# A conditioned two-layer block: weight rounding, row norms and layer gates put in another order

## The reference, cut to what matters

```python
def _weight_quant(w):
    scale = 1.0 / clip(mean(abs(w)), 1e-05)
    return clip(round(w * scale), -1, 1) / scale
def _bitlinear(x, w, nw, b=None):
    xn = x * rsqrt(mean(square(x)) + 1e-08) * nw
    y = act_quant(xn) @ weight_quant(w).T              # act_quant: 8 bits by the row's maximum
    return y if b is None else y + b
# the conditioning chain, on 2 rows
h = _bitlinear(silu(c), wa0, na0)
h = _hgrn_mlp(h, wa1, na1, wa2, na2)
h = _rmsnorm(_bitlinear(h, wa3, na3, ba3), wr, 1e-06)
s_msa, sc_msa, g_msa, s_mlp, sc_mlp, g_mlp = split(_bitlinear(h, wa4, na4, ba4), 6)
# the first mixer
mx = _layernorm(x) * (1 + sc_msa) + s_msa
f = sigmoid(_bitlinear(mx, wf, nf))
i = silu(_bitlinear(mx, wi, ni)) * (1 - f)
o = _rmsnorm(scan(i, f), gn) * silu(_bitlinear(mx, wg, ng))
x = x + g_msa * _bitlinear(o, wo, no_)
mlp_in = _layernorm(x) * (1 + sc_mlp) + s_mlp
x = x + g_mlp * _hgrn_mlp(mlp_in, wm1, nm1, wm2, nm2)  # then layer 1: attention and MLP
# layer 1: mod = silu(c) @ Wada + bada; sh_a, sc_a, gt_a, sh_m, sc_m, gt_m = split(mod, 6)
```

## Time and profile before

| | us |
|---|---|
| median of 3 runs | 249.67 (249.2 to 250.05) |
| the profiled execution | 250.22 |
| its span in the trace | 248.0 |
| VectorE, TensorE, ScalarE, GpSimd busy | 173.0, 180.0, 152.2, 78.4 |

### The profile page before, as it was taken

The page is one execution under the profiler, slowest core; times in us unless marked ns, Lnnn a source line. Parts: engine busy times, 40 slices in busy tenths (PEclk is TensorE's granted clock), DMA queues, the critical chain, the costliest instruction groups (busy, mean ns, idle before and its releaser), DMA issues.

```text
span 248.0 us, 4504 instructions
## 1 busy us (share of the span) xinstructions
PE 180.0 (73%) x1635; PEld 106.3 (43%) x1639; DVE 173.0 (70%) x501; ACT 152.2 (61%) x334; POOL 78.4 (32%) x116
## 2 busy tenths in 40 slices
PE   0223269586494659755976897699999999889894
PEld 0202226454341313311643454367556655544663
DVE  1778787999986496697697479578778777462511
ACT  3767983679724757695515642567657755976241
POOL 9261520404713013378313978011001101130120
PEclk9999999779859779995999799599999999999999
DMA  5999000000000000000000333124000000000011
GB/s 145 409 425 348 4 0 0 0 3 1 0 0 1 3 0 0 1 0 0 0 3 13 106 79 62 41 31 66 5 2 5 3 5 5 1 4 0 0 45 42
DMA packets 4635, 11.50 MB, mean 46 GB/s; under 512 B 1283, under 2 KB 2788, under 8 KB 3974
## 3 DMA queue, kind: packets, MB, share of 16 engines
q1 hardware_dynamic: 3654, 10.03, 12.1%
q0 software_dynamic: 960, 1.19, 2.0%
HBM read 8.23 MB, written 0.52 MB: 35 GB/s over the span
## 4 chain that ended last, share of the span: by engine, by line
DVE 35%; PE 29%; ACT 14%; POOL 13%; issue 6%; DMA 1%; SPq 0%; DVEq 0%; ACTq 0%; POOLq 0%
DVE negmax L1351 7%; PE ps L1747 6%; POOL uh L465 4%; PE ps L1506 4%; POOL KS L348 3%; ACT PT L793 2%; PE ps L1686 2%; PE ps L1783 2%; ACT xhat L683 2%; DVE mx L1243 2%; DVE u L1130 2%; POOL rms L405 2%; PE ps L1727 2%; PE ps L1777 1%; PE ps L1474 1%
## 5 line engine op out<-in xcount | busy, mean ns | idle before, releaser
L1351 DVE TENSOR_REDUCE negmax<-ps 128x1 f32<-128x384 f32 (+3 forms) x96 | 51.2, 593 | 14.1 <-PE ps L1688 13.8
L793 ACT ACTIVATE PT<-ps 128x1024 f32<-128x1024 f32 x40 | 39.5, 1031 | 20.4 <-PE ps L1733 20.3
L1517 PE MATMUL ps<-k_b 128*128 128x512 bf16 x114 | 33.4, 453 | 9.5 <-DVE prod L1289 4.4
L1686 PE MATMUL ps<-KS,QS 48*128 48x128 bf16 (+3 forms) x128 | 31.4, 315 | 1.6 <-DVE negmax L1351 0.8
L1727 PE MATMUL ps<-QS,KS 51*128 51x512 bf16 (+3 forms) x128 | 24.6, 311 | 1.8 <-DMA QS<-nmT 1.8
L405 POOL TENSOR_TENSOR rstd<-veps,mhalf 128x4 f32<-128x4 f32 x8 | 9.8, 1220 | 50.7 <-DVE veps L912 40.8
L1517 PEld LDWEIGHTS ps<-k_b 128*128 128x128 bf16 x114 | 12.7, 115 | 27.7 <-issue 8.9
L1687 PE MATMUL ps<-k_b 64*128 64x128 bf16 x128 | 23.8, 225 | 0.0
L1688 PE MATMUL ps<-k_b 64*128 64x64 bf16 x128 | 21.4, 195 | 0.0
L1747 PE MATMUL ps<-PT,V 128*9 128x512 f32 (+3 forms) x256 | 20.4, 434 | 0.0
L1733 PE MATMUL ps<-k_b 64*128 64x128 bf16 x128 | 18.7, 223 | 0.0
(11 more groups left out here) (237 smaller groups left out, 457.2 us busy)
## 6 DMA issues: line engine op xcount, KB each, us to landing
w<-in_wa SPq DMA_DIRECT2D x2, 1152.0 KB, 9.5
lw<-in_l_w SPq DMA_DIRECT2D x1, 1280.0 KB
brow<-in_bcast_rows SPq DMA_DIRECT2D x1, 1152.0 KB, 15.4
mw<-in_main_w SPq DMA_DIRECT2D x1, 1024.0 KB, 12.5
KS<-part POOLq DMA_DIRECT2D x12, 64.0 KB, 3.4
QS<-part SPq DMA_DIRECT2D x12, 64.0 KB
cw<-in_cond_w SPq DMA_DIRECT2D x1, 576.0 KB, 4.5
xs<-in_x SPq DMA_DIRECT2D x1, 512.0 KB, 6.2
```

The source lines that it names most:

```text
L793: nc.scalar.activation(PT[n % 2][:, s, :], bank(2 * (use % 2), 2), ACT.Exp).then_inc(S["p_ready"], 1)
L1351: V.tensor_reduce(negmax[n % 2][:, qt, h0:h0 + nh], bank(S_BANKS[k % 3])[:, 0:nh * w].rearrange("p (h w) -> p h w", w=w), AX.X, ALU.max, n ...
L1517: T.matmul(bank(bk).rearrange("p (r n) -> p r n", n=P), ident_b, ident_b.unsqueeze(1).to_broadcast([P, NT, P]), start=True, stop=True)
L1686: T.matmul(dst, QS[b][rows, h, tok(qt)], KS[b][rows, h, 0:w], start=True, stop=False)
```

## The change

Weights and norms: `wa2` is rounded on ScalarE like `wa1`; of `wa4` chunks 0 to 3 are rounded and clipped as before, chunks 4 and 5 get only the first ScalarE pass, and VectorE clamps them and takes MAGIC off. GpSimd keeps only the comparison for `wa3`, and VectorE zeroes `picks` first of all. The means of `wi` to `wo` are made ahead of the `wa4` rounding, without the half means (`main_means`). `xhat` of the first mixer comes from ScalarE (`centre`), after statistics that VectorE takes for both b during the conditioning. Layer shifts and gates stand behind the first mixer products of b = 0 in the place of its idle products, `normed_squares(1)` behind the sigmoids of b = 0, `picks` and the magnitudes of `wm1` and `wm2` ahead of the second output norm, and `main_clip(4, 6)` behind the second modulation of b = 0.

```diff
-W4_ROUND = (0, 1, 2, 5, 4)
-W4_STEPS = (3,)
+W4_ROUND = (0, 1, 2, 3)
+W4_CLAMP = (4, 5)
...
             c_root(0, 0)
-            nc.gpsimd.memset(picks[:, :, :, :, :].bitcast(FP32), 0.0).then_inc(S["picks_init"], 1)
...
-            for c in W4_STEPS:
-                low(w4q[:, c, :], w4[:, c, :], "wa4")
...
+            act.wait_ge(S["wa2_inv"], 1)
+            wa2 = slice(*CW["wa2"])
+            nc.scalar.activation(cw[:, wa2], cw[:, wa2], ACT.Copy, bias=MAGIC, scale=winv[:, 2:3]
+                                 ).then_inc(S["wa2_magic"], 1)
+            act.wait_ge(S["wa2_magic"], 1)
+            nc.scalar.activation(cwq[:, wa2], cw[:, wa2], ACT.Copy, bias=-MAGIC).then_inc(S["wa2_rounded"], 1)
...
+            for c in W4_CLAMP:
+                scaled4(c)
+
+            def centre(b, n, done):
+
+                act.wait_ge(S["ln_bias"], n)
+                for t in range(b * NT, b * NT + NT):
+                    ins = nc.scalar.activation(xhat[:, t, :], xs[:, t, :], ACT.Identity, bias=nbias[:, t:t + 1],
+                                               scale=rstd[:, t:t + 1])
+                ins.then_inc(done, 1)
...
+            centre(0, 1, S["xhat_first"])
+            round_main(0, 4)
+            act.wait_ge(S["wsum_ready"], 14)
             normed_squares(0)
...
+            centre(1, 2, S["xhat_first"])
...
-                if b == 0:
-                    normed_squares(1)
                 for j in (1, 0, 2):
                     gate(b, j)
                 act.wait_ge(S["fT_pe"], b + 1)
                 nc.scalar.activation(fT[b][:, :], bank(4 * b + 2), ACT.Copy).then_inc(S["fT_ready"], 1)
...
+                if b == 0:
+                    normed_squares(1)
+                    act.wait_ge(S["mod_pe"], 1)
+                    nc.scalar.activation(modraw[:, :], bank(4)[:, 16:16 + 4 * B], ACT.Copy).then_inc(S["mod_copied"], 1)
+                    act.wait_ge(S["gate_pe"], 1)
+                    nc.scalar.activation(gates[:, :, :, :].rearrange("p i b d -> p (i b d)"), bank(7), ACT.Copy
+                                         ).then_inc(S["mod_copied"], 1)
...
+            def main_means(first, n, total, bk):
+
+                cols = slice(first, first + n)
+                a = KC["count"][0]
+                dve.wait_ge(S["wtot_pe"], total)
+                then(V.tensor_tensor(wraw[:, cols], bank(bk)[:, cols], k_f[:, a + first:a + first + n], ALU.mult))
+                then(V.tensor_scalar(wmean[:, cols], wraw[:, cols], CLIP, None, ALU.max))
+                V.reciprocal(winv[:, cols], wmean[:, cols]).then_inc(S["inv_ready"], 1)
...
+            def clamp4(c):
+                dve.wait_ge(S["w4_magic"], c + 1)
+                then(V.tensor_scalar(w4[:, c, :], w4[:, c, :], MAGIC - 1.0, MAGIC + 1.0, ALU.max, ALU.min))
+                V.tensor_scalar(w4q[:, c, :], w4[:, c, :], MAGIC, None, ALU.subtract).then_inc(S["w4_ready"], 1)
...
+            V.memset(picks[:, :, :, :, :].bitcast(FP32), 0.0).then_inc(S["picks_init"], 1)
...
-            high4(3)
-            ln_apply(b0_tiles, 1)
-            clip4(5)
-            clip4(4)
+            bn(b1_tiles[3:])
+            ln_variance(b1_tiles, 1e-6)
+            clip4(3)
+            clamp4(4)
+            clamp4(5)
...
+            main_means(8, 2, 6, 2)
...
-            main_clip(4, 6)
...
                 modulate(b, 3)
                 if b == 0:
                     ln_bias(1, B + 2)
+                    main_clip(4, 6)
...
             for b in range(B):
+                if b:
+                    pe.wait_ge(S["mod_copied"], 2)
...
                 else:
-                    idle_products(8, 2)
+                    layer_shifts()
                 pe.wait_ge(S["sig_ready"], 3 * b + 1)
                 to_columns(bank(4 * b + 2), lambda t: fg[b][:, 1, t, :], S["fT_pe"])
                 if b == 0:
-                    pe.wait_ge(S["mod_copied"], 2)
-                    idle_products(6, 4)
+                    layer_gates()
```

More of the change, by code:

```diff
@@ L1011, in _ @@
             a, z = CW["wa2"]
-            high(cwq[:, a:z], cw[:, a:z], "wa2", 1)
+            dve.wait_ge(S["wa2_rounded"], 1)
+            then(V.tensor_scalar(cwq[:, a:z], cwq[:, a:z], -1.0, 1.0, ALU.max, ALU.min))
             V.tensor_copy(k_b[:, 0:P], k_f[:, 0:P]).then_inc(S["masks_ready"], 1)
@@ L1403, in _, with totals @@
             T = nc.tensor
-            def totals(first, n, sums):
+            def totals(first, n, sums, bk=7):
                 pe.wait_ge(S["wsum_ready"], sums)
-                T.matmul(bank(7)[:, first:first + n], ones[:, :], wsum[:, first:first + n], start=True, stop=True
+                T.matmul(bank(bk)[:, first:first + n], ones[:, :], wsum[:, first:first + n], start=True, stop=True
                          ).then_inc(S["wtot_pe"], 1)
@@ L1468, in parameter_product @@
                 z = min(a + 512, OUT6)
-                for c in W4_ORDER:
-                    if c in W4_STEPS:
-                        pe.wait_ge(S["w4_stepped"], W4_STEPS.index(c) + 1)
-                    else:
-                        pe.wait_ge(S["w4_ready"], W4_ROUND.index(c) + 1)
-                    ins = T.matmul(bank(PARAM_BANKS[b] + a // 512)[:, 0:z - a], cxq[:, c, b:b + 1].to_broadcast([P, P]),
-                                   w4q[:, c, a:z], start=(c == W4_ORDER[0]), stop=(c == W4_ORDER[-1]))
@@ L1489, in _ @@
-            ins.then_inc(S["mod_pe"], 1)
-            a = LW["Wada"][0]
-            g0 = R1["bgate"][0]
-            for i, j in enumerate((2, 5)):
-                for b in range(B):
-                    dst = bank(3)[:, (2 * i + b) * D:(2 * i + b + 1) * D]
-                    T.matmul(dst, scT[:, b:b + 1].to_broadcast([P, P]), lw[:, a + j * D:a + (j + 1) * D],
-                             start=True, stop=False)
-                    ins = T.matmul(dst, ones[0:1, :], row1[:, g0 + i * D:g0 + (i + 1) * D], start=False, stop=True)
@@ L1499, in _ @@
-            ins.then_inc(S["gate_pe"], 1)
-            pe.wait_ge(S["half_ready"], 5)
-            totals(8, 2, 16)
+                for c in range(OC):
+                    pe.wait_ge(S["w4_ready"], c + 1)
+                    ins = T.matmul(bank(PARAM_BANKS[b][a // 512])[:, 0:z - a], cxq[:, c, b:b + 1].to_broadcast([P, P]),
+                                   w4q[:, c, a:z], start=(c == 0), stop=(c == OC - 1))
+                ins.then_inc(S["c_mm"], 1)
+            for b in range(B):
+                parameter_product(b, 0)
+                parameter_product(b, 512)
@@ new lines, in layer_shifts, with layer_gates @@
+            def layer_shifts():
+                pe.wait_ge(S["ld_l1"], 32)
+                pe.wait_ge(S["silu_c"], 2)
+                a = LW["Wada"][0]
+                for i, j in enumerate((0, 1, 3, 4)):
+                    ins = T.matmul(bank(4)[:, 16 + B * i:16 + B * (i + 1)], lw[:, a + j * D:a + (j + 1) * D], scT[:, :],
+                                   start=True, stop=True)
+                ins.then_inc(S["mod_pe"], 1)
+            def layer_gates():
+                a = LW["Wada"][0]
+                g0 = R1["bgate"][0]
+                pe.wait_ge(S["inv_ready"], 2)
+                for i, j in enumerate((2, 5)):
+                    for b in range(B):
+                        dst = bank(7)[:, (2 * i + b) * D:(2 * i + b + 1) * D]
+                        T.matmul(dst, scT[:, b:b + 1].to_broadcast([P, P]), lw[:, a + j * D:a + (j + 1) * D],
+                                 start=True, stop=False)
+                        ins = T.matmul(dst, ones[0:1, :], row1[:, g0 + i * D:g0 + (i + 1) * D], start=False, stop=True)
+                ins.then_inc(S["gate_pe"], 1)
```

139 lines of the change are left out of this document (58 added, 81 removed).

## The result

The changed kernel takes 242.19 us (median of 4 runs, 242.02 to 243.1) against 249.86 for the kernel before: ratio 0.9702, 95% interval 0.9672 to 0.9732. That is 7.67 us faster. The profiled execution took 243.1 (span 241.3) against 250.22 (span 248.0), 7.12 less.

What follows compares the result with a forecast made beforehand. No engine but one chain of waits hopping between engines was taken as the bound; 1.3 in the mixer and 3.55 at its end, 4.85, gave 245.4 for the profiled execution and 244.8 on the median, range 242.6 to 247.4.

Steps and rivals of the forecast that it cites:

- parts 1, 2 and 4: Part 1, part 2, and at the mixer's end a residual no longer waiting for ScalarE's rounding and the clip, -3.55.
- the contention: Conditioning: small VectorE instructions no longer stretched beside GpSimd, -0.4 without its memset and -1.1 without its `wa4` comparison.
- part 1: Conditioning up to the first parameters: 1.7 gained at the last rounding, -1.0 left at the first parameters.
- part 2: VectorE, b = 0: second parameters, statistics and means leave the stretch before rounding, 3.1; rounding at 43.5, -4.1.
- the new wait: First mixer, b = 1: VectorE waits 2.7 us for ScalarE's squares, handing back 1.6; `m_mean` comes 2.5 earlier.
- part 3: First mixer, b = 1: wait for squares hands back 1.6, slow transposes cost 1.2; layer gates don't hold the clock.
- clock term: TensorE's transposes of b = 1 in the first mixer take 3.08 instead of 1.88 at the lower clock, +1.2.
- the mixer's gain of 1.3: First mixer: 4.1 gained in b = 0, less 1.6 for the wait and 1.2 for the slower clock.
- rival 1: First mixer: layer gates at 1.2 GHz take 6.0 us, end at 57, hold b = 1, cost 1.6; 246.4, chance 0.27.
- rival 2: TensorE stays at 2.4 GHz through b = 1: 243.6, idle products another 1.8 at most; chance 0.18.
- Rival 3: Idle products between `wo` products and the transposes at 102.88 become the bound, 1.9 later; 251.6, chance 0.05.
- Rival 4: Mixer's end: the residual waits for something else, centring or products, losing the gain there; 248.4 or no change, chance 0.06.

Runs made afterwards that it cites:

- e7: Changed kernel with two unused GpSimd instructions added, a zeroing of 128x1536 float32 and a comparison of 128x768; 243.96 us, ratio 0.9748.
- e1: Kernel before with only the clip of `wm1` and `wm2` moved behind the second modulation of b = 0; 247.26 us, ratio 0.9889.
- e2: Changed kernel with the clip of `wm1` and `wm2` put back ahead of the residual; 246.26 us, ratio 0.9852.
- e9: Changed kernel with 8 idle products added between the parameter products and the transposes of b = 0; 241.52 us, ratio 0.9666.
- e8: Changed kernel with squares of b = 1 ahead of the sigmoids of b = 0 and layer gates split in two, off that stretch; 240.24 us, ratio 0.9604.
- e3: Kernel before without the 8 idle products ahead of the last scan columns; 249.28 us, ratio 0.9978.
- e4: Changed kernel without the 8 idle products ahead of the last scan columns; 242.82 us, ratio 0.9697.
- e5: Changed kernel with the squares of b = 1 put back ahead of the sigmoids of b = 0; 244.39 us, ratio 0.9774.
- e6: Changed kernel with layer shift and gate products back behind the parameter products and 8 idle products back in b = 0; 243.81 us, ratio 0.9749.

## Why the prediction was right or wrong

**Right: parts 1, 2 and 4.** The last conditioning rounding gained 1.69 (forecast 1.7), the first parameters 1.28 (1.0); the clamp pass is 0.55 (taken at 0.6), and e7 shows the contention at 1.11, somewhat under the 1.5 forecast for comparison and zeroing together. The rounding of b = 0 starts at 43.43 (43.5); that this is so near is in part luck, as part 1 gave 0.28 more than forecast and part 2 0.15 less (2.95 of 3.1). At the mixer's end 3.65 was won (3.55), and e1 and e2 show it from both sides, with `picks` as the next thing that is late. The three pieces of part 2 are read from the two traces alone; no run puts them back.

**Right in mechanism: the new wait.** VectorE waits 2.58 for the squares (2.7), and the norms of b = 1 gain 2.91 (2.5).

**Wrong: part 3's clock term and what it left at nothing, and with them the mixer's gain of 1.3.** It measured 3.08 at the output rows. Two pieces make up the 1.8.

1. The transposes of b = 1 are slow, as forecast (2.82), but I charged their whole 1.2 to the path. From the norms of b = 1 to its scan the kernel before takes 13.63 (56.00 to 69.63) and e9, with transposes as slow (2.79), 13.82; e8 takes 13.84. So slow transposes cost 0.2: VectorE still has the silu products of b = 0 ahead of it then, and doesn't wait ahead of the first scan in e8 or e9. The changed kernel takes 14.51. Its other 0.7 is rival 1's term, which the forecast put at nothing: TensorE waits for the copy of the gates. The profile puts the wait of 0.69 at 57.28 down to VectorE's rounding, but TensorE needs only the first half of that to start: in e9 it starts 1.03 behind the rounding's start, which would be 56.64 here. It shows as the 0.53 that VectorE idles ahead of the first scan. So 1.0 of my 1.2 was not there, and 0.7 that I had left out was; that the two partly cancel is luck. With the norms 0.41 earlier than forecast, the scan stands at 2.03 instead of 1.3.
2. The 8 idle products at the earlier trace rows that took 3.62 lay on the path of the kernel before: 1.04 by the trace of e3. I saw them, priced them at up to 1.8, and left them to rival 2, tied to a TensorE that stays at 2.4 GHz all through b = 1. They were not tied to that. The clock was low through the transposes and products of b = 1 and came back at 63, in time for them. Forecast and rival 2 were not two cases but two terms with their own conditions.

Behind the mixer the chain moved as a whole, as forecast: VectorE is 6.73 ahead at the residual and still 6.73 ahead behind the MLP (127.85 against 134.58). The last 0.39 of the profiled gain lies after that, and its cause stays open.

**Between the profiled execution and the median** lies another 0.5: 243.1 is the slowest of the changed kernel's 4 runs and 0.91 above their median, while 250.22 is 0.36 above the median of the kernel before. e2 runs the same code up to the cast, its clock falls later, and it shows how much that can move:

```profile
42.75:45.00 2.25, 0.55 (x4) 0.42 (x4) 2.13 (x12) 1.94 (x6) 0.00 (x0) 1.00 0.00 0
...
49.00:52.00 3.00, 3.00 (x20) 2.39 (x19) 1.50 (x1) 3.00 (x14) 0.00 (x0) 1.00 0.00 0
```

The clock is at 1.00 in stretches where the profiled execution of the changed kernel has 0.50, the gates are copied by 54.2 and don't hold b = 1, and the cast starts at 79.18 instead of 80.41. That the three faster runs of the changed kernel went this way isn't shown, for they left no trace, and an earlier scan alone doesn't make a fast run: e4's profiled execution has its scan 0.9 earlier than the changed kernel's and took 244.43. I subtracted 0.55 for the profiled execution of before, and didn't allow for the other one.

**The rivals.** Rival 1 happened in part: the gates took 5.7 us at 1.2 GHz and ended at 56.6, almost exactly as worked out (6.0, 57), but cost 0.7 and not 1.6. My price took the start of the rounding for the start of TensorE's work, which comes about 1.0 later. e5 shows what the gates hold without the wait for the squares, and e6 that they don't hold the clock, as part 3 said. Rival 2's condition didn't hold in the profiled execution (1.2 GHz until 63), but its idle products paid all the same. Rival 3 did not happen: 19 of the idle products behind `wo` took 5.4 and 18 took 4.1, and VectorE's or ScalarE's results ended the waits around them. Rival 4 is refuted by e1 and e2.

## What to carry to other kernels

A delay on one engine is charged to the path only after one has followed what the waiting engine still has queued: here slow transposes charged at 1.2 us cost 0.2, and a wait of 2.6 us taken away alone gave nothing, because a second bound lay right behind it. A wait on several results is put down to one of them by the profile; a variant in which another of them comes early (e9) shows which one held it. Where two waits cover each other, take both away in one kernel (e8: 2.45 us, when one alone lost 1.8). And filler products that hold a clock up should have a price for the case that the clock is down: what they last beyond the next result that TensorE waits for.

## What the runs showed of the hardware

- **The clock differs between executions of the same code.** Up to the cast the code of e2 and of the changed kernel is the same, and the granted clock falls at 45.4 in one and at 42.7 in the other; the cast comes 1.2 us earlier in e2. The Trainium skill, "TensorE: Matmul & The Clock Gate", Part 1, says that the number of slow products varies between runs of one kernel; the traces agree, here in the middle of a kernel. By the same part the throttled clock is the default and activity releases it. e9 agrees, with 1.88 for the transposes behind 8 products and 2.79 behind idle time; in e6 the clock fell at 44.8 all the same, while the layer products ran.
- **The printed granted clock doesn't show the first rise.** In e8 the printed clock is 1.00 while the first half of the layer gates runs:

```profile
30.90:33.50 2.60, 2.60 (x9) 1.78 (x8) 2.05 (x13) 2.60 (x5) 0.40 (x1) 1.00 0.00 0
```

And yet a pair of products there takes 0.79, as at 1.2 GHz in the changed kernel (the row at 55.80), and the same pair of the second half 0.48. That TensorE ran at 1.2 GHz at first is read from these durations; e8's timeline:

```profile
31.42 0.79 PE L1509 MATMUL ps<-row,ones 1*128 1x128 f32 x2
...
40.56 0.48 PE L1509 MATMUL ps<-row,ones 1*128 1x128 f32 x2
```

- **GpSimd slows some small VectorE instructions by about half a microsecond, not by its own length.** In e7 a 2x1 instruction that starts 0.18 us behind a GpSimd comparison of 2.23 us takes 0.75 instead of 0.15; two later ones beside the same comparison take 0.66 and 0.47 instead of 0.22 and 0.16, while three in between keep their 0.15, 0.27 and 0.20. The Trainium skill, "SBUF — State Buffer", Who interferes with whom, calls the shared ports an exclusive lock for the whole instruction; by that the first would have ended near 26.5, and it ended at 25.2. The profile's spans of GpSimd are rough, so the comparison's own end is uncertain; the 0.75 is not, and the measurement decides.
